# A fused attention and expert layer on one core: where VectorE adds the fourth down tile of each quad

## The reference, cut to what matters

```python
# B, S, D = 8, 256, 512; all in float32
x = x + tanh(g_xattn[0]) * xattn(layernorm(x), ctx, ctx, wq, wk, wv, wo)
x = x + tanh(g_ffn[0]) * ffn(layernorm(x), gate_w, mask_up_w, gate_proj_w, up_proj_w, down_proj_w, inv_map)

def ffn(x, ...):                       # x: N = 2048 tokens, H = 512
    scores = softmax(x @ gate_w.T)     # 64 experts, the best 8 kept
    w_e = zeros.at[topk_idx].add(topk_w)
    flat = w_e[:, inv_map]             # 8 groups of 8
    scalar = flat.sum(-1)
    soft = softmax(where(flat == 0, -1e9, flat), axis=-1)
    xg = x[:, None, :] + einsum('ngi,ghi->ngh', soft, mask_up_w)
    g = einsum('ngh,gih->ngi', xg, gate_proj_w)      # inner size 352
    u = einsum('ngh,gih->ngi', xg, up_proj_w)
    d = einsum('ngi,ghi->ngh', silu(g) * u, down_proj_w)
    return einsum('ng,ngh->nh', scalar, d)
```

## Time and profile before

| | |
|---|---|
| median of 3 runs | 1068.88 us (1067.83 to 1069.12) |
| the profiled execution | 1067.69 us, its span 1065.9 us |
| TensorE matmuls busy | 1049.2 us, 98% |
| weight loads busy | 891.4 us, 84% |
| VectorE busy | 742.7 us, 70% |
| GpSimd busy | 614.3 us, 58% |
| ScalarE busy | 388.9 us, 36% |

### The profile page before, as it was taken

How to read it: one execution, slowest core, us unless ns; L and a number is a source line. 1 busy time by engine, 2 the same in 40 slices (tenths; PEclk the granted TensorE clock), 3 DMA queues, 4 the chain that set the end, 5 groups by cost and what they waited for, 6 DMA issues and landing times.

```text
span 1065.9 us, 14507 instructions
## 1 busy us (share of the span) xinstructions
PE 1049.2 (98%) x5388; PEld 891.4 (84%) x5388; DVE 742.7 (70%) x1314; ACT 388.9 (36%) x651; POOL 614.3 (58%) x545
## 2 busy tenths in 40 slices
PE   8999999999999899999999999999999999999998
PEld 8988988998988688888887888888888888888886
DVE  7874665676678588787789888765666665666555
ACT  5334323434434334243424343333332333333331
POOL 1312102223336766768778888678668677668661
PEclk9999999999999999999999999999999999999999
DMA  9212216354895214224235433493321211221202
GB/s 333 76 38 99 63 48 149 66 151 122 237 283 192 90 36 48 74 77 35 87 114 61 130 107 104 163 301 114 114 74 47 75 58 44 74 74 48 75 28 79
DMA packets 114133, 111.64 MB, mean 105 GB/s; under 512 B 20880, under 2 KB 96400, under 8 KB 114064
## 3 DMA queue, kind: packets, MB, share of 16 engines
q1 hardware_dynamic: 113696, 110.58, 35.8%
q10 hardware_dynamic: 368, 0.15, 0.1%
HBM read 79.05 MB, written 31.65 MB: 104 GB/s over the span
## 4 chain that ended last, share of the span: by engine, by line
PE 84%; DVE 9%; issue 2%; POOL 2%; DMA 1%; ACT 1%; SPq 0%; DVEq 0%
PE bank L84 37%; PE bank L1679 32%; PE bank L1493 8%; PE bank L1685 3%; PE bank L1512 2%; DMA w_raw<-in_w_qkvo 1%; PE bank L1693 1%; DVE tmp L1345 1%; DVE a_stack L1336 1%; POOL wgu_lo L661 1%; DVE a_stack L1334 1%; DVE a_tmp L1328 1%; DVE tmp L1461 1%; DVE tmp L1371 1%; DVE xres L1352 1%
## 5 line engine op out<-in xcount | busy, mean ns | idle before, releaser
L1679 PE MATMUL bank<-x2t,wgu_hi 128*128 128x512 f32 x1144 | 353.0, 390 | 0.0
L661 POOL TENSOR_TENSOR wgu_lo<-wgu_raw,wgu_hi 128x768 fp32r<-128x768 f32 (+2 forms) x143 | 213.5, 1504 | 83.5 <-ACT wgu_hi L812 81.9
L1679 PEld LDWEIGHTS bank<-x2t,wgu_hi 128*128 128x128 f32 x1144 | 214.8, 188 | 44.3
L1679 PE MATMUL bank<-x2t,wgu_lo 128*128 128x512 f32 x572 | 224.2, 392 | 2.2 <-DVE tmp L1405 1.9
L812 ACT CAST wgu_hi<-wgu_raw 128x512 fp32r<-128x512 f32 (+1 forms) x129 | 93.7, 727 | 222.6 <-PE bank L1685 186.1
L1352 DVE TENSOR_TENSOR xres<-xres,bank 128x512 f32<-128x512 f32 x176 | 120.2, 683 | 54.8 <-PE bank L84 54.3
L84 PE MATMUL bank<-wd_hi,at_second 128*128 128x512 f32 x336 | 131.5, 391 | 0.0
L1679 PEld LDWEIGHTS bank<-x2t,wgu_lo 128*128 128x128 f32 x572 | 107.5, 188 | 25.4 <-issue 2.7
L84 PE MATMUL bank<-wd_hi,at_first 128*128 128x512 f32 x256 | 100.5, 393 | 3.3 <-issue 3.3
L1345 DVE TENSOR_TENSOR tmp<-tmp,scalars 128x512 f32<-128x512 f32 x88 | 100.4, 1141 | 3.3 <-DMA scalars<-scals 0.3
L633 POOL TENSOR_TENSOR kt_lo<-ctxt_raw,kt_hi 128x256 fp32r<-128x256 f32 x32 | 23.5, 762 | 136.8 <-ACT kt_hi L837 136.8
(11 more groups left out here) (218 smaller groups left out, 2247.9 us busy)
## 6 DMA issues: line engine op xcount, KB each, us to landing
wgu_raw<-in_w_gate_up SPq DMA_DIRECT2D x43, 512.0 KB, 4.1
wd_raw<-in_w_down SPq DMA_DIRECT2D x22, 512.0 KB, 5.1
a_stacks<-a_stack SPq DMA_DIRECT2D x22, 192.0 KB, 1.9
a_stack<-a_stacks SPq DMA_DIRECT2D x22, 192.0 KB, 4.0
ctxt_raw<-in_ctx_t SPq DMA_DIRECT2D x8, 512.0 KB, 11.3
ctx_raw<-in_ctx SPq DMA_DIRECT2D x8, 512.0 KB, 8.0
x<-x_raw SPq DMA_DIRECT2D x8, 512.0 KB, 7.8
sums_raw<-x SPq DMA_DIRECT2D x16, 256.0 KB, 3.6
```

Of the source, the lines that this page charges most:

```text
L661: last = nc.gpsimd.tensor_tensor(wgu_lo[:, part], raw_of(quad)[:, part], f32(wgu_hi[:, part]), ALU.subtract)
L1679: last = nc.tensor.matmul(out_bank[:], stationary, moving, start=begins and n == 0, stop=n == len(pairs) - 1, skip_group_check=True)
```

## The change

`late_sum` is removed. VectorE now adds all four down tiles of a quad (quads 2 to 43) one behind the other where it added the first three, that is behind L1464 and ahead of `second_activations`. Before, the fourth addition stood behind the next quad's second sum (and A tile) in 33 quads (2, 6, 10, 11, 13 to 16, 18 to 42), and behind the own second activations in the other nine (3, 4, 5, 7, 8, 9, 12, 17, 43). The order of the other four engines is the same, row for row.

```diff
--- before.py
+++ after.py
@@ -65,11 +65,6 @@
 def early_tiles(q):
 
     return 0 if q <= 2 or q == QUADS - 1 else 2
-
-
-def late_sum(q):
-
-    return 2 <= q < QUADS - 1 and q + 1 not in ROUTED_ON_ODD
 
 
 def split_products(hi_l, lo_l, hi_r, lo_r, tiles):
@@ -1385,8 +1380,6 @@
                         out_lo(B - 1)
                     if quad.first_pass:
                         a_tile(quad)
-                if late_sum(q - 1):
-                    add_down(below - 1)
                 if q == 0:
                     late_x2_lo(B - 2, 4)
                 if q == 2:
@@ -1465,15 +1458,13 @@
                 if q == 0:
                     a_tile(quads[1])
                 if q >= 2:
-                    for n in range(early, 3):
+                    for n in range(early, 4):
                         add_down(below + n)
                 if q == 1:
                     second_sum(quads[2])
                     a_tile(quads[2])
                 if q >= 1:
                     second_activations(quad)
-                if q >= 2 and not late_sum(q):
-                    add_down(below + 3)
             for n in range(UNIT_TILES * (UNITS - 1), UNIT_TILES * UNITS):
                 add_down(n)
```

## The result

The change made the kernel slower, by more than forecast. In the comparison the medians were 1071.64 us with the change (11 runs, 1069.92 to 1072.64) and 1068.39 us without (11 runs, 1067.00 to 1070.01): ratio 1.0028, 95% interval 1.0018 to 1.0039, or +3.0 us with +1.9 to +4.2. The time lies in the stated range, but the change does not lie where most of the chance stood: forecast were +1.95 us and, with 0.53, "within 0.2%".

A forecast was written before the change was run, and what follows sets the result against it. TensorE was taken as the bound, busy 344.58 of 345.00 us in the second pass. Terms 1.55 - 0.84 + 0.44 + 0.4 + 0.4 = +1.95 us gave 1069.6, forecast as 1070.8 us from the runs' higher median; range 1068.9 to 1072.9.

The forecast's parts named there:

- second pass, odd quads: Quads 21 to 41: late scaling delays ScalarE's cast, GpSimd and the next down tile's weight load; 11 x 0.14 = +1.55 us.
- second pass, even quads: Scaling and second sum up to 1 us later, covered by 2.7 us of TensorE matmuls; no cost.
- gate of quad 13: First pass: TensorE's stack transposes no longer wait for quad 12's last addition; a gain of 0.84 us, whole.
- chain of quad 14: First pass: quad 13's later L1371 delays GpSimd and quad 14's first down tile, counted in full; +0.44 us.
- quads 12, 16 (with 17), 18: Quads 12, 16 and 18: same GpSimd chain with about 0.7 us of slack, 0 to 0.25 each; +0.4 us in all.
- A tile and the rest (quads 4, 5, 8, 9, 15, 19 to 21): First pass: longer VectorE queue ahead of the A tile at two places, small gains at quads 4 and 8; net +0.4 us.
- tail: Quad 43: one bank freed 0.1 us earlier, the next held 0.1 us longer; 0.
- a cover that holds: Rival: the second pass hides the 0.19 us delay, leaving only the first pass's +0.4, 1069.3 us; chance 0.22.
- About 0.9 us in place of 0.42: Sign expected in the profile after: a longer wait at the first down tile of quad 14.
- the first rival: The rival "Slower, by collisions": later second activations fall behind GpSimd instructions; +2.0 us, 1072.8 us, chance 0.26.
- The sign that I had set for being wrong: Wrong if the second pass keeps its length, or if waits for `a_stack` grow by over 1.3 us.
- Slower, by collisions: Rival: second activations fall behind GpSimd instructions in the first pass; +2.0 us on the forecast, 1072.8 us; chance 0.26.

The follow-up runs named there:

- e5: The change plus, in even quads, ScalarE casting the down weights ahead of the second activations, against the kernel before: 1066.89 us against 1068.41, ratio 0.9987.
- e8: Addition moved in the second pass alone, plus one extra VectorE copy ahead of the second activations in odd quads from 23 on: one run, 1073.14 us.
- e4: Every fourth addition put behind its own quad's second activations, ahead of the next second sum, against the kernel before: 1068.52 us, ratio 0.9992.
- e7: As e3, with GpSimd's low part of quad 14's first weight group cut into three instructions: 1068.12 us, ratio 0.9993 against the kernel before.
- e3: Addition moved only in the nine quads where it stood behind the own second activations, against the kernel before: 1068.24 us, ratio 0.9993.
- e1: Additions moved ahead of the second activations in the second pass alone (quads 22 to 43), against the kernel before: 1070.82 us against 1068.97, ratio 1.0024.
- e6: Kernel before with only ScalarE's two casts exchanged in even quads, additions not moved: 1068.95 us, ratio 1.0008.
- e9: The change, exchanged casts, and GpSimd's first low parts cut in three in quads 14, 16, 18, 20, against the kernel before: 1064.94 us against 1068.77, ratio 0.9952.
- e10: Exchanged casts and GpSimd's low parts cut as in e9, but additions not moved, against the kernel before: 1066.73 us, ratio 0.9974.

## Why the prediction was right in one half and wrong in the other

The second pass came out as described; the first did not, and its sum of +0.4 was +2.1.

| term | forecast | measured (steps) |
|---|---|---|
| second pass, odd quads | +1.55 | +1.37 |
| second pass, even quads | 0 | 0 |
| gate of quad 13 | -0.84 | +0.04 |
| chain of quad 14 | +0.44 | +0.76 |
| quads 12, 16 (with 17), 18 | +0.4 | +0.68, +0.56, +0.47 |
| A tile and the rest (quads 4, 5, 8, 9, 15, 19 to 21) | +0.4 | -0.43 |
| tail | 0 | -0.06 |
| sum | +1.95 | +3.39 |

That the time still fell into the stated range is partly luck. The terms missed by -0.18 (second pass), +0.88 (gate), +0.32 (quad 14), +1.31 (quads 12, 16 and 18) and -0.83 (A tile and the rest), which partly cancel, and the forecast of the time started from a median 0.5 us above the one that the comparison gave.

**Second pass: right in mechanism, and nearly in size.** The addition that waits for its tile, the scaling's end 0.04 us ahead of the cast and 0.34 us between load and matmul are as stated. Measured are eleven steps of 0.113 to 0.141, 0.125 on average where 0.14 was written, and removing the chain (e5) or lengthening it (e8) moves exactly this number. The chance of 0.22 for a cover that holds rested on TensorE's showing no wait there, and that sign cannot decide: in after its busy time is 345.00 out of 345.00 us although each pair of quads is longer by 0.12 us.

**The gate: the step "-0.84 us, whole" failed.** The addition did move and the wait is gone, as forecast, but a wait of 0.91 us for the A tile came in its place, and the step is +0.04. The prediction's next sentence, "Late next there is VectorE's A tile, which shows no wait at this quad", was read from a trace in which TensorE stands still for 0.84 us just there. I asked whether the A tile waits now, not how near it is when TensorE comes 0.84 us earlier, nor what TensorE's progress starts on GpSimd. The whole cast collided (0.36 to 1.95 us).

**Quad 12: the chain was right, its end was not.** I followed it to the down tile, at 0 to 0.25 us. It ends earlier, at the A tile. First VectorE and GpSimd before, then the same and TensorE in after:

```profile
528.61 0.67 DVE L1328 TENSOR_TENSOR a_tmp<-a_tmp 128x128 f32<-128x128 f32 x1
...
527.83 2.60 POOL L707 TENSOR_TENSOR wd_lo<-wd_raw,wd_hi 128x512 fp32r<-128x512 f32 x2
```

```profile
529.40 1.35 DVE L1323 TENSOR_TENSOR a_tmp<-a_tmp 128x128 f32<-128x128 f32 x1
530.88 1.24 DVE L1329 CAST a_stack<-a_tmp 128x384 fp32r<-128x384 f32 x1
532.16 1.52 DVE L1331 TENSOR_TENSOR a_stack<-a_tmp,a_stack 32x384 fp32r<-32x384 f32 x1
...
529.30 2.61 POOL L702 TENSOR_TENSOR wd_lo<-wd_raw,wd_hi 128x512 fp32r<-128x512 f32 x2 [0.65 <-ACT wd_hi L916]
...
533.74 0.73 PE L1676 MATMUL bank<-soft_t,a_stack 128*128 128x512 f32 x2 [0.73 <-DVE a_stack L1331]
```

Before, GpSimd began L707 without a wait, 0.78 us ahead of VectorE's L1328. Now it waits 0.65 us for ScalarE's cast and begins 0.10 us ahead of L1323. Each of the three A tile instructions ends only when the GpSimd instruction beside it does (1.35, 1.24, 1.52 us), so a late start of GpSimd is handed on whole: GpSimd starts 1.47 us later than before, of which 0.79 are the lag of the whole program there (the quad's first addition at 524.21 against 523.42), so 0.68 are new, and so is TensorE's step. With the casts exchanged the step is -0.01. Quads 16 to 18 lose 1.03 us in all and +0.03 with the casts exchanged. In quad 17 the cast takes 1.78 us beside L656, as in quad 13.

**Quad 14: the right chain, at half its size.** "About 0.9 us in place of 0.42" at the first down tile did not come: the row says 0.47. But TensorE itself comes there later, since it now waits 0.36 us for the A tile just ahead. Starts compared with starts give the size. The down tile starts at 571.06 where it was 568.65, 2.41 us later, of which 1.51 were there at quad 13's soft product: 0.90 us, where 0.44 was forecast. VectorE's second activations and GpSimd beside them, after (the earlier trace rows has L1371 before, 561.24 and 0.69 us), then the down tile:

```profile
563.27 1.07 DVE L1366 TENSOR_TENSOR tmp<-tmp 128x512 f32<-128x512 f32 x1
...
563.05 0.74 POOL L672 TENSOR_TENSOR sums_raw<-sums_raw 128x256 f32<-128x256 f32 x1
...
571.06 0.47 PE L79 MATMUL bank<-wd_hi,at_first 128*128 128x512 f32 x1 [0.47 <-issue]
```

Against quad 13's lag L1366 starts 0.52 us late: 0.10 because the first addition (562.08) does, and 0.42 by the moved addition, as forecast. But it then falls behind GpSimd's L672 and takes 1.07 us instead of 0.69. These 0.38 us, the first rival's mechanism, are what the term lacked. Both the A tile and GpSimd's low parts stand behind it, so both come 0.90 us late, and the A tile's wait comes first. The exchange of the casts therefore does not take the step of quad 14 away (+0.68), only what follows it.

**A listed idle time is not the price of a wait.** TensorE ahead of quad 14's soft product, after:

```profile
568.88 0.61 PE L1670 MATMUL bank<-x2t,wgu_hi 128*128 128x512 f32 x2
...
569.86 0.73 PE L1676 MATMUL bank<-soft_t,a_stack 128*128 128x512 f32 x2 [0.36 <-DVE a_stack L1331]
```

Two matmuls take 0.45 us in the queue, so the product could have started at 569.33; it started 0.53 us later, while 0.36 us are listed. The idle time counts from the end of the last matmul (0.39 us long), though the next could start 0.23 us behind its start: each wait costs 0.16 us more than its row says. It fits the gains in quads 4 and 8, where waits of 0.17 and 0.20 us for the A tile went and the steps are -0.33 and -0.38. I had allowed 0.17 each.

**The A tile term: the wrong mechanism.** I charged +0.4 us for a longer queue ahead of the tile. The longer queue costs nothing in all (e4, +1.15 and -1.21); the additions there even gave a gain in quads 4, 5, 8 and 9. The sign that I had set for being wrong, waits for `a_stack` that grow by over 1.3 us, came true: +1.9.

**The rivals.** "Slower, by collisions" named the right resource, at +2.0 us beyond the forecast, where +1.4 came. Its instructions, second activations that fall behind one of GpSimd's, were right only at quad 14, with 0.38 us. At quads 12, 13 and 17 it was the A tile's that were held, at 13 by the gate's own gain. Without the collision at quad 13 the sum would have been 0.69 us less (e7's step against e3's). The rival counted on the second activations alone, which have two SBUF inputs. The traces show a cast with a single SBUF input going from 0.36 to 1.95 us beside GpSimd. The Trainium skill (SBUF — State Buffer, "Who interferes with whom") says of VectorE's copies and casts that they can enter a mode that uses the port pair shared with GpSimd, and then contend with it, when their operands meet certain conditions. The trace agrees.

## What to carry to other kernels

When an edit removes a wait of the bounding engine, redo the reading of the next two waits with that engine moved forward: what its progress starts on the other engines may land on the instruction that it needs next. In each queue, put work that waits for nothing ahead of work that waits for another engine, if a longer chain hangs on it; the early addition was a loss of 3 us with the casts in one order, and part of a gain with the other. Neither edit was a gain by itself, so each was worth testing with the other. A busy share of 100% doesn't exclude losses of 0.13 us per pair of quads; starts compared with starts show them, and so does the idle time of the weight loads (0.27 us).

## What the runs showed of the hardware that I had not expected

**Delays come in steps.** A VectorE instruction held by one of GpSimd ended a fixed time behind it, whenever it had started: the cast 0.21 us (551.61 against 551.40), the 128x128 operation 0.15 us (549.53 against 549.38), the 128x512 one with two SBUF inputs 0.54 us (845.95 against 845.41). In the traces of all twelve kernels the held casts end 0.21 to 0.22 us behind. Of the same casts, those that started 0.11 to 0.2 us ahead of GpSimd's instruction kept their 0.36 us. So which of two starts 0.1 us ahead decides over about 1.6 us, and cutting GpSimd's instruction in three bounds the loss (0.85 us).

**TensorE's clock after three waits.** At about 348 to 361 us TensorE waits 0.94, 1.50 and 2.83 us within 14 us, in all kernels alike. In some executions the granted clock then fell, in others not. The stretch from 360 to 370 us, before and then e5_weights_cast_first, with the clock as third number from the end, and one pair of matmuls of each:

```profile
360.00:370.00 10.00, 8.90 (x32) 7.25 (x33) 3.83 (x6) 1.43 (x3) 8.04 (x11) 0.83 0.30 105
...
363.18 0.63 PE L84 MATMUL bank<-wd_hi,at_first 128*128 128x512 f32 x1
363.61 0.63 PE L84 MATMUL bank<-wd_lo,at_first 128*128 128x512 f32 x1
```

```profile
360.00:370.00 10.00, 7.79 (x34) 6.49 (x35) 5.64 (x8) 1.84 (x3) 9.69 (x12) 1.00 0.28 96
...
363.67 0.40 PE L89 MATMUL bank<-wd_hi,at_first 128*128 128x512 f32 x1
363.90 0.39 PE L89 MATMUL bank<-wd_lo,at_first 128*128 128x512 f32 x1
```

Before, the matmuls stand 0.43 us apart for about 3 us, the 1.2 GHz level, against 0.23 us at 2.4 GHz. It costs 1.6 us: in the executions where the clock held (e1, e5, e6, e8), quad 3's step is -1.6. One and the same kernel can have either: the mean granted clock of the runs of after goes from 0.996 to 1.000. It is part of the scatter of the runs behind the medians. What decides it stays open.

The difference ahead of quad 3 goes with the clock in part. It arises in the first 35 us, where the programs are the same, and then stays to quad 3 (e7 alone loses 1.0 us more). The stretch from 10 to 20 us, before and then after:

```profile
10.00:20.00 10.00, 9.26 (x77) 9.29 (x78) 8.76 (x16) 5.73 (x8) 1.47 (x1) 1.00 1.07 368
```

```profile
10.00:20.00 10.00, 8.16 (x56) 8.20 (x57) 8.19 (x12) 6.92 (x10) 1.46 (x1) 0.83 1.07 367
```

Where the clock is 1.00 in this stretch, TensorE is 0.5 us ahead (e9) and 0.7 us behind (e10) the kernel before at 35 us. Where it is 0.83, it is 1.1 to 1.9 us behind, and in e8, with 0.66, 3.2 us. The clock is not all of it: at 12 us after is 1.7 us behind, but so is e10 by 1.4 us, whose clock holds. Why TensorE comes late there was not followed up.
